# A decoder layer on one core: the cross norm's statistics, its powers and xn's transposes moved to later places

## The chip, the core and the metric

One core of a Trainium2 chip runs the whole layer in one program. The metric is the device time of one execution in microseconds; lower is better. The engines are TensorE (PE in the profile, its weight loads PEld), VectorE (DVE), ScalarE (ACT), GpSimd (POOL) and SyncE (SP, which here only issues DMAs). Each engine takes its instructions in the order of the program, and they meet through semaphores.

## The reference, cut to what is computed

B = 16 sequences of T = 256 tokens with D = 256 features and H = 16 heads of 16.

```
x = layernorm(x + attn(x))                 # causal self attention, q and k rms-normed and rotated
x = layernorm(x + xattn(x, ctx, mask))     # causal cross attention on ctx
x = layernorm(x + ffn(x))                  # ffn(x) = heavy(x) + light(x); with n = 256 all tokens are routed
feedforward: h = x / max(|x|, 1e-12) * sqrt(D) * gamma;  gelu(h @ w1.T + b1) @ w2.T + b2
```

The steps around the change are the second layer norm and the normalisation at the head of the FFN: `x2 = (y2 - mean) * rstd`, then `xn = x2 * rr2`, where `rr2` comes from the variance and `rstd` alone (`ss2 = var * rstd * rstd`, then a power of -1/2).

## The kernel before

The kernel is software-pipelined over the 16 sequences. `iterations` calls `step(i)` for i from -2 to 19 on each engine, and in a step four sequences are at work: `s = i` (self attention), `c = i - 1` (cross attention), `f = i - 2` (end of cross attention, second norm, xn) and `l = i - 3` (FFN). `live(b)` is true where the sequence exists. The sequence f exists together with s in the 14 steps i = 2 to 15, and without s in the steps 16 and 17.

On TensorE a step has four stages of 16 heads each: self scores, `scores(1, s, h)`; cross scores, `scores(2, c, h)`; transposed self scores, `scores_t(1, s, h)`; transposed cross scores, `scores_t(2, c, h)`. Everything else that TensorE does is put ahead of a given head by a list of positions: `phase` issues, at each h, first the "others" of that position and then the head. Three PSUM banks go round as a ring for the heads: `wait_ring` makes a head wait until the maximum (first two stages) or the exponential (last two) of the head three earlier has read its bank. `values(a, b, gr)` multiplies four masked heads by v; in the third stage it stands ahead of the heads 7, 11 and 15 (`VALUES_AFTER = 7`, every 4), and it waits for the masks of its four heads. `ffn_out` matmuls fill the third stage ahead of the heads 0 to 10.

A head of the third stage goes through three engines: TensorE scores it, ScalarE takes its exponential (`exponential`, line 768), GpSimd zeroes the causal half (`mask_probs`, line 1311), TensorE multiplies it by v (`values`). `mask_probs(a, b, between)` can run another function ahead of the mask of a given head: `between[h]()`.

The second norm runs like this. VectorE adds the residual (`add_residual(2, f, ...)`), takes the statistics (`statistics(2, f)`: two bn_stats, line 1022, two bn_aggr, line 1028), GpSimd adds epsilon and takes the power (`inverse_deviation(2, f)`, lines 1269 and 1290) and derives the second factor (`inverse_norm2(f)`, lines 1276, 1279, 1282 and 1290), VectorE scales (`layer_norm(2, f)`, line 1043; `scale2(f)`, line 1052), TensorE transposes xn (`transpose_xn`, line 397), ScalarE copies the high half from the bank (`copy_xn`), VectorE takes the low half (`low_xn`, line 1112). All in one step. Both halves feed `hidden` of the next step; `qk1(i + 2, 1)` at head 6 of the fourth stage waits for `low_xn` as well, since both use bank 7.

In the kernel before, the statistics stand ahead of the maximum of cross head 6 in the second stage (`STAT2_AT = 6`); GpSimd does `inverse_deviation(2, f)` and `inverse_norm2(f)` ahead of its first self mask; VectorE's order behind the cross maxima (`maxima`, `max_parts`) is layer_norm, max_t, the split of the next q (`split(1, i + 1, 0, 0)`), scale2, the split of the next k, low_xn, the third residual and its statistics, and the division of the self heads (`divide_pair`); TensorE transposes xn ahead of head 12 of the third stage (`XNT_AT = 12`); ScalarE copies it behind the exponential of self head 13.

Of the kernel before, what the change touches and what calls it, by code (L numbers as in the profile page):

```python
# [59 lines left out]
FCH = 9  # L60
# [5 lines left out]
def build(nc, io):  # L66
# [4 lines left out]
    with ctx:  # L71
# [144 lines left out]
        def live(b):  # L216

            return not isinstance(b, int) or 0 <= b < B
# [149 lines left out]
        def _(pe):  # L368
# [257 lines left out]
            def step(i):  # L626
                s, c, f, l = i, i - 1, i - 2, i - 3

                others = {}

                def add(at, fn, *args):
                    others.setdefault(at, []).append(lambda: fn(*args))

                if live(c):
                    add(X1T_AT, transpose_x1, c)
                if live(f):
                    add(OUT2_AT[0], values, 2, f, NG - 1)
                if live(c):
                    add(Q2_AT, q2, c)
                if live(f):  # L640
                    add(OUT2_AT[1], out_tokens, f)
                    add(OUT2_AT[2], out_dims, f)
                    add(OUT2_AT[3], out_proj, 2, f)
                if live(l):
                    for j in range(FCH):
                        add(HIDDEN_AT[j], hidden, l, j)
                phase((lambda h: scores(1, s, h)) if live(s) else None, others)

                others = {}
                if first(i + 1):  # L650
                    add(0, qk1, i + 2, 0)
                    add(0, qk1, i + 2, 1)
                if live(i + 1):
                    add(QKT_AT, transpose_qk1, i + 1)
                if live(s):
                    add(MAX1_AT, transpose_max, 1, s)
                if live(c):
                    add(V2_AT, v2, c)
                if live(l):
                    for j in range(FCH):  # L660
                        add(FFN0_AT[j], ffn_out, l, 0, j)
                phase((lambda h: scores(2, c, h)) if live(c) else None, others)

                others = {}
                if live(c):
                    add(MAX2_AT, transpose_max, 2, c)
                if live(f):
                    add(XNT_AT, transpose_xn, f)
                if live(l):
                    for j in range(FCH):  # L670
                        add(FFN1_AT[j], ffn_out, l, 1, j)
                if live(s):
                    for gr in range(NG - 1):
                        add(HG * gr + VALUES_AFTER, values, 1, s, gr)
                phase((lambda h: scores_t(1, s, h)) if live(s) else None, others)

                others = {}
                if live(s):
                    add(K2_AT, k2, s)
                    add(OUT1_AT[0], values, 1, s, NG - 1)  # L680
                if live(i + 2) and not first(i + 1):
                    add(QK1_AT[0], qk1, i + 2, 0)
                if live(i + 2) and not first(i + 1):
                    add(QK1_AT[1], qk1, i + 2, 1)
                if live(s):
                    add(OUT1_AT[1], out_proj, 1, s)
                if live(i + 2):
                    add(V1_AT, v1, i + 2)
                if live(c):
                    for gr in range(NG - 1):  # L690
                        add(HG * gr + VALUES_AFTER, values, 2, c, gr)
                phase((lambda h: scores_t(2, c, h)) if live(c) else None, others)
# [7 lines left out]
        def _(act):  # L700
# [92 lines left out]
            def step(i):  # L793
# [38 lines left out]
                for h in range(H):  # L832
                    if live(s):
                        if h % HG == 0 and h >= 2 * HG:
                            copy_group(1, s, h // HG - 2)
                        exponential(1, s, h)
                    if h == COPY_XN_AT and live(f):
                        copy_xn(f)

                for h in range(H):  # L840
                    if live(s):
                        if h == COPY1_AT[0]:
                            copy_group(1, s, NG - 2)
                        if h == COPY1_AT[1]:
                            high_part(2, s, 1, 0)
                        if h == COPY1_AT[2]:
                            copy_group(1, s, NG - 1)
                    for t in range(TT):
                        if h == SQ_AT[t] and live(i + 2) and not first(i + 1):
                            squares(i + 2, t)  # L850
                    if live(c):
                        if h % HG == 0 and h >= 2 * HG:
                            copy_group(2, c, h // HG - 2)
                        exponential(2, c, h)
                    if h == COPY_V1_AT and live(i + 2):
                        copy_v(1, i + 2)
# [44 lines left out]
        def _(dve):  # L901
# [213 lines left out]
            def step(i):  # L1115
# [40 lines left out]
                def statistics_cross():  # L1156
                    if live(f):
                        statistics(2, f)

                if live(c):  # L1160
                    maxima(2, c, {RESID2_AT: residual_cross, MAXT_AT: max_rows, STAT2_AT: statistics_cross})
                    max_parts(2, c)
                else:
                    residual_cross()
                    max_rows()
                    statistics_cross()

                if live(f):
                    layer_norm(2, f)
                if live(c):  # L1170
                    max_t(2, c)
                if live(i + 1):
                    split(1, i + 1, 0, 0)
                if live(f):
                    scale2(f)
                if live(i + 1):
                    split(1, i + 1, 1, 1)
                if first(i):
                    scale_w1()
                if live(f):  # L1180
                    low_xn(f)
                if live(l):
                    dve.wait_ge(s_x2b, l + 1)
                    add_residual(3, l, FFN_BANK, x2b)
# [1 line left out]

                if live(s):
                    divide_pair(s, 0)
                    take_rest(2, s, 1, 0)
                    divide_pair(s, 1)  # L1190
                    split_rest(2, s, 1, 0)
# [58 lines left out]
        def _(pool):  # L1250
# [63 lines left out]
            def step(i):  # L1314
# [39 lines left out]
                if live(i - 4) and i - 4 < B - 1:  # L1354
                    layer_norm3(i - 4)

                if live(f):
                    inverse_deviation(2, f)
                    inverse_norm2(f)

                if live(s):
                    mask_probs(1, s, {})

                roots = {}
                if live(l):
# [36 lines left out]
HIDDEN_AT = (6, 6, 8, 8, 11, 11, 14, 14, 16)  # L1402
QKT_AT, MAX1_AT, V2_AT = 2, 4, 6
FFN0_AT = (3, 5, 7, 8, 9, 10, 11, 12, 13)
MAX2_AT, XNT_AT = 5, 12
FFN1_AT = (0, 1, 2, 3, 4, 6, 8, 9, 10)
K2_AT, OUT1_AT, QK1_AT, V1_AT = 1, (3, 9), (3, 6), 13

MIDQ_AT, COPY2_AT, COPY_XN_AT, COPY_V1_AT = 1, 4, 13, 15
COPY1_AT, SQ_AT = (0, 3, 3), (5, 7)  # L1410
QN_AT, NORM2_AT, SPLITQ_AT, LOWQ_AT, RESID2_AT, MAXT_AT, STAT2_AT = (1, 2), 5, 6, 8, 1, 3, 6
RSTD3_AT, RSTD1_AT = 3, 13
NSTK = (None, 2 * len(TERMS_Q), 2 * len(TERMS_Q) + 1)
NEWTON = 3 + 3 * 3
N_SELF, N_CROSS, N_FFN = 3, 5, 8
# [44 lines left out]
```

## Time and profile before

| | |
|---|---|
| median of 3 runs | 978.58 us (974.46 to 981.06) |
| profiled execution | 978.16 us, of which its span is 976.4 us |
| busy share of the span | PE 91%, PEld 71%, DVE 74%, ACT 51%, POOL 55% |
| granted TensorE clock, mean | 0.960 of full speed |

The span reaches from the first to the last instruction. The shares are means over a start, some 13 steps that look alike, and an end. Times in rows are microseconds from the start of the span; a row of the timeline gives start, duration, engine, line, operation, tiles and, in brackets, the idle time just before it and what ended it. A count such as x4 merges instructions that follow each other.

### The profile page before, as it was taken

Reading aid. Unit: us, or ns where it says so; the run is one execution under the profiler, and the core shown is the slowest. Engines: PE = TensorE matmul, PEld = TensorE weight load, DVE = VectorE, ACT = ScalarE, POOL = GpSimd, SP = SyncE. Lnnn points to the kernel's source line nnn. Section 1 sums busy time; section 2 is a strip of 40 time slices with the busy share of each in tenths; the row PEclk is TensorE's granted clock in tenths of the full one; section 3 lists DMA queues with packets and bytes.
Section 4 is the critical chain, followed back from the end, with each engine's and each line's share of the span. In section 5 each row is a group of like instructions: output and inputs, shape, how many; then the busy total and the mean of one; then the engine's idle time right before and its main releaser. Section 6 shows DMA issues by size and latency. Waiting matters only on the chain. (4 is left out here: it accounts for less than half of the span.)

```text
span 976.4 us, 21698 instructions
## 1 busy us (share of the span) xinstructions
PE 888.3 (91%) x7712; PEld 689.7 (71%) x7712; DVE 725.3 (74%) x1764; ACT 496.8 (51%) x1063; POOL 537.9 (55%) x1047
## 2 busy tenths in 40 slices
PE   3367897999999999999999999999999999999886
PEld 2335565787868787777878787877778686767576
DVE  7788687878788878879787888788887877663411
ACT  1132444646475655656464756556464746455332
POOL 7554465646564756656565647657565656162421
PEclk9669898999999999999999999999999999999888
DMA  3794383727476654818275666738283656613000
GB/s 110 120 173 68 52 110 50 106 33 109 51 100 78 98 78 65 111 37 110 34 119 59 100 78 80 97 54 107 44 109 42 95 72 88 77 31 49 14 11 21
DMA packets 79644, 74.22 MB, mean 76 GB/s; under 512 B 8593, under 2 KB 78897, under 8 KB 79537
## 3 DMA queue, kind: packets, MB, share of 16 engines
q1 hardware_dynamic: 75008, 68.11, 50.5%
q10 hardware_dynamic: 4528, 4.73, 1.9%
q8 instruction: 61, 1.00, 0.5%
q14 instruction: 47, 0.38, 0.2%
HBM read 17.49 MB, written 4.20 MB: 22 GB/s over the span
## 5 line engine op out<-in xcount | busy, mean ns | idle before, releaser
L768 ACT ACTIVATE pr<-bank 128x384 f32<-128x384 f32 x512 | 240.0, 500 | 188.1 <-PE bank L370 187.0
L946 DVE TENSOR_REDUCE mx<-bank 128x3 f32<-128x384 f32 x512 | 266.4, 552 | 89.7 <-PE bank L370 87.5
L1311 POOL TENSOR_SCALAR_AFFINE_SELECT pr<-pr 128x256 f32<-128x256 f32 x512 | 222.1, 448 | 132.3 <-ACT pr L768 130.1
L370 PE MATMUL bank<-w,g 128*128 128x256 f32 x576 | 170.8, 389 | 1.1 <-ACT g L780 1.1
L370 PE MATMUL bank<-cmaskb,idb 128*128 128x256 bf16 x512 | 143.3, 280 | 27.7 <-DMA stk2k<-nat1k 13.7
L780 ACT ACTIVATE g<-bank,b 128x256 f32<-128x256 f32 x144 | 67.8, 473 | 83.5 <-PE bank L370 83.2
L1335 POOL TENSOR_TENSOR xTlow<-xT,xThigh 128x512 fp32r<-128x512 f32 x16 | 20.8, 1301 | 149.8 <-ACT xThigh L702 149.8
L370 PEld LDWEIGHTS bank<-w,g 128*128 128x128 f32 x576 | 89.6, 190 | 5.2 <-ACT g L780 1.5
L370 PEld LDWEIGHTS bank<-cmaskb,idb 128*128 128x128 bf16 x512 | 50.1, 98 | 50.5 <-DVE mx L946 22.5
L370 PE MATMUL bank<-stk2k,stk2q 97*128 97x128 bf16 (+1 forms) x512 | 85.1, 253 | 0.0
L370 PE MATMUL bank<-stk1q,stk1k 100*128 100x256 bf16 (+1 forms) x512 | 80.1, 254 | 2.4 <-DMA stk1q<-mT 1.0
L370 PE MATMUL bank<-stk1k,stk1q 97*128 97x128 bf16 (+1 forms) x512 | 80.6, 246 | 0.0
L370 PE MATMUL bank<-stk2q,stk2k 100*128 100x256 bf16 (+1 forms) x512 | 69.1, 255 | 5.3 <-DMA stk2q<-mT 3.6
L264 POOL TENSOR_TENSOR qc<-qn,ropeC 128x256 f32<-128x256 f32 x60 | 49.3, 821 | 43.8 <-DVE qn L1087 43.8
L370 PE MATMUL bank<-xnh,w1h 128*128 128x256 f32 x288 | 66.6, 313 | 3.7 <-DVE y L1015 2.1
L370 PEld LDWEIGHTS bank<-stk1q,stk1k 100*128 100x128 bf16 x512 | 42.4, 100 | 36.7 <-issue 7.5
L370 PEld LDWEIGHTS bank<-stk2k,stk2q 97*128 97x128 bf16 x512 | 51.9, 101 | 19.3
L370 PE MATMUL bank<-wo,onT 128*128 128x256 f32 x256 | 63.0, 390 | 1.3 <-DVE onT L997 1.3
L370 PE MATMUL bank<-pr,va 128*32 128x256 f32 (+1 forms) x1024 | 57.5, 344 | 3.7 <-POOL pr L1311 3.5
L370 PE MATMUL bank<-xnl,w1h 128*128 128x256 f32 x288 | 58.3, 284 | 0.0
L370 PE MATMUL bank<-xnh,w1l 128*128 128x256 f32 x288 | 58.2, 284 | 0.0
L370 PEld LDWEIGHTS bank<-stk2q,stk2k 100*128 100x128 bf16 x512 | 36.4, 100 | 30.8 <-issue 15.1
(166 smaller groups left out, 1832.5 us busy)
## 6 DMA issues: line engine op xcount, KB each, us to landing
stk1q<-nat1q SPq DMA_DIRECT2D x90, 128.0 KB, 4.5
stk1k<-nat1k SPq DMA_DIRECT2D x90, 128.0 KB, 5.4
stk2k<-nat2k SPq DMA_DIRECT2D x90, 128.0 KB, 4.6
stk2q<-nat2q SPq DMA_DIRECT2D x90, 128.0 KB, 5.7
xT<-in_xT SPq DMA_DIRECT2D x16, 256.0 KB, 5.9
ctxT<-in_ctxT SPq DMA_DIRECT2D x16, 256.0 KB, 6.0
x<-in_x SPq DMA_DIRECT2D x16, 256.0 KB, 5.7
out_x<-x SPq DMA_DIRECT2D x16, 256.0 KB, 2.2
```

The costliest lines, as they stand in the source:

```text
L264: ops.tensor_tensor(qc[:, t, s * D:(s + 1) * D].rearrange("p (h d) -> p h d", d=HD), qn[:, t, s * D:(s + 1) * D].rearrange("p (h d) -> p h ...
L370: return nc.tensor.matmul(out, lhsT, rhs, start=start, stop=stop, skip_group_check=check)
L768: nc.scalar.activation(pr[:, h % (2 * HG), :], ring_bank("T", a, b, h)[:, 0:3 * P], ACT.Exp, scale=HD ** -0.5)\
L780: nc.scalar.activation(g[:, j, :], bank[HIDDEN_BANK[j % 2]][:, 0:T], ACT.Gelu, bias=b1[:, j:j + 1])\
L946: V.tensor_reduce(mx3[:, h, :], scored[:, 0:3 * P].rearrange("p (k t) -> p k t", k=3), AX.X, ALU.max, negate=True).then_inc(s_mx[a], 1)
L1311: G.affine_select(out=slot, in_=slot, compare_op=ALU.is_ge, fill=0.0, base=0, pattern=[[0, 2], [1, P]], channel_multiplier=-1).then_inc(s_ ...
L1335: G.tensor_tensor(xTp[1][:, :, :], xT[:, :, :], xTp[0][:, :, :].bitcast(f32), ALU.subtract)\
```

## The change

- VectorE: `statistics_cross` is called behind `max_parts(2, c)` and no longer between the maxima; `layer_norm(2, f)` goes behind `max_t` and the split of the next q, `scale2(f)` behind the split of the next k, `low_xn(f)` behind the third norm's statistics and `divide_pair(s, 0)`.
- GpSimd: `inverse_deviation(2, f)` goes from ahead of the self masks to ahead of the mask of self head 2, `inverse_norm2(f)` to ahead of that of head 5. Where there is no s, both stay where they were.
- TensorE: `transpose_xn(f)` goes from ahead of head 12 of the third stage to the head of the fourth, ahead of its first head. Where there is no s it stays at position 12.
- ScalarE: `copy_xn(f)` goes from behind self exponential 13 to ahead of cross exponential 1; where there is no s, to the first position of the self loop.

No operation is added or taken away, and no DMA is touched.

```diff
 # TensorE
-                if live(f):
-                    add(XNT_AT, transpose_xn, f)
+                if live(f) and not live(s):
+                    add(FCH + 3, transpose_xn, f)
 ...
                 others = {}
+                if live(f) and live(s):
+                    add(XNT_AT, transpose_xn, f)
 # ScalarE
-                    if h == COPY_XN_AT and live(f):
+                    if h == 0 and live(f) and not live(s):
                         copy_xn(f)
                 for h in range(H):
+                    if live(f) and live(s) and h == COPY_XN_AT:
+                        copy_xn(f)
 # VectorE
-                    maxima(2, c, {RESID2_AT: residual_cross, MAXT_AT: max_rows, STAT2_AT: statistics_cross})
+                    maxima(2, c, {RESID2_AT: residual_cross, MAXT_AT: max_rows})
                     max_parts(2, c)
                 else:
                     residual_cross()
                     max_rows()
-                    statistics_cross()
-                if live(f):
-                    layer_norm(2, f)
+                statistics_cross()
                 if live(c):
                     max_t(2, c)
                 if live(i + 1):
                     split(1, i + 1, 0, 0)
                 if live(f):
-                    scale2(f)
+                    layer_norm(2, f)
                 if live(i + 1):
                     split(1, i + 1, 1, 1)
+                if live(f):
+                    scale2(f)
                 if first(i):
                     scale_w1()
-                if live(f):
-                    low_xn(f)
                 if live(l):
                     ...
                 if live(s):
                     divide_pair(s, 0)
+                if live(f):
+                    low_xn(f)
+                if live(s):
                     take_rest(2, s, 1, 0)
 # GpSimd
+                roots = {}
                 if live(f):
-                    inverse_deviation(2, f)
-                    inverse_norm2(f)
-
+                    roots[RSTD2_AT[0]] = lambda: inverse_deviation(2, f)
+                    roots[RSTD2_AT[1]] = lambda: inverse_norm2(f)
                 if live(s):
-                    mask_probs(1, s, {})
+                    mask_probs(1, s, roots)
+                else:
+                    for h in sorted(roots):
+                        roots[h]()
 # positions
-MAX2_AT, XNT_AT = 5, 12
+MAX2_AT, XNT_AT = 5, 0
-MIDQ_AT, COPY2_AT, COPY_XN_AT, COPY_V1_AT = 1, 4, 13, 15
+MIDQ_AT, COPY2_AT, COPY_XN_AT, COPY_V1_AT = 1, 4, 1, 15
-RSTD3_AT, RSTD1_AT = 3, 13
+RSTD2_AT, RSTD3_AT, RSTD1_AT = (2, 5), 3, 13
```

## Rows read from the trace of the kernel before

**Rows 1.** Windows: third stage of step 7, busy time by engine, granted clock.

```profile
429.42:439.72 10.30, 10.15 (x104) 6.83 (x102) 7.32 (x19) 7.54 (x18) 8.58 (x20) 1.00 0.42 81
```

**Rows 2.** Waits of PE over ten like steps, 240.6 to 781.3.

```profile
PE bank L397 <- DVE x L1043: 2.9, 10, 0.3
PE bank L370 <- DVE mx L946: 1.9, 10, 0.3
PE bank L370 <- POOL pr L1311: 0.6, 3, 0.2
```

**Rows 3.** Timeline of DVE in step 7, second and third stage.

```profile
422.66 0.73 DVE L1022 BATCH_NORM_STATS2 st<-y 128x6 f32<-128x256 f32 x2
423.32 0.29 DVE L1028 BATCH_NORM_AGGREGATE mv<-st 128x2 f32<-128x6 f32 x2
...
427.92 0.56 DVE L946 TENSOR_REDUCE mx<-bank 128x3 f32<-128x384 f32 x1 [0.15 <-PE bank L370]
...
431.23 0.75 DVE L1043 TENSOR_SCALAR x<-y,mv,rstd 128x256 f32<-128x256 f32 x2
...
434.17 0.77 DVE L931 TENSOR_TENSOR nat1q<-rest,nat1q 128x512 bf16<-128x512 f32 x1
```

**Rows 4.** Timeline of POOL in step 7, third stage.

```profile
429.28 0.22 POOL L1269 TENSOR_SCALAR ve<-mv 128x2 f32<-128x2 f32 x1
429.58 0.71 POOL L1290 TENSOR_TENSOR rstd<-ve,minus_half 128x2 f32<-128x2 f32 x1
430.36 0.19 POOL L1276 TENSOR_TENSOR part<-mv,rstd 128x2 f32<-128x2 f32 x1
...
431.32 0.72 POOL L1290 TENSOR_TENSOR rr<-ssm,minus_half 128x2 f32<-128x2 f32 x1
432.01 0.41 POOL L1311 TENSOR_SCALAR_AFFINE_SELECT pr<-pr 128x256 f32<-128x256 f32 x1
...
433.09 0.41 POOL L1311 TENSOR_SCALAR_AFFINE_SELECT pr<-pr 128x256 f32<-128x256 f32 x1
...
434.36 0.85 POOL L1311 TENSOR_SCALAR_AFFINE_SELECT pr<-pr 128x256 f32<-128x256 f32 x1
...
436.58 0.57 POOL L1311 TENSOR_SCALAR_AFFINE_SELECT pr<-pr 128x256 f32<-128x256 f32 x1 [0.24 <-ACT pr L768]
...
437.24 0.72 POOL L1311 TENSOR_SCALAR_AFFINE_SELECT pr<-pr 128x256 f32<-128x256 f32 x1
...
438.29 0.41 POOL L1311 TENSOR_SCALAR_AFFINE_SELECT pr<-pr 128x256 f32<-128x256 f32 x1 [0.34 <-ACT pr L768]
```

**Rows 5.** Timeline of ACT in step 7: the exponential of self head 11.

```profile
437.74 0.49 ACT L768 ACTIVATE pr<-bank 128x384 f32<-128x384 f32 x1 [0.57 <-PE bank L370]
```

**Rows 6.** Timeline of PE in step 7: self values, xn's transposes.

```profile
433.55 0.86 PE L370 MATMUL bank<-pr,va1b 128*32 128x256 f32 x16
...
436.57 0.86 PE L370 MATMUL bank<-pr,va1b 128*32 128x256 f32 x16
...
437.54 0.61 PE L397 MATMUL bank<-idf,xn 128*128 128x128 f32 x4
437.98 0.66 PE L370 MATMUL bank<-stk1q,stk1k 100*128 100x256 bf16 x6
438.75 0.86 PE L370 MATMUL bank<-pr,va1b 128*32 128x256 f32 x16
```

**Rows 7.** Timeline of step 16, the first without self heads: PE, then DVE.

```profile
915.03 0.60 PE L397 MATMUL bank<-idf,xn 128*128 128x128 f32 x4
916.59 0.67 PE L370 MATMUL bank<-stk1q,stk1k 100*128 100x256 bf16 x6 [0.97 <-DMA stk1q<-mT]
...
912.84 0.73 DVE L1043 TENSOR_SCALAR x<-y,mv,rstd 128x256 f32<-128x256 f32 x2
```

**Rows 8.** Windows of step 15, fourth stage: before the clock falls, and after.

```profile
871.30:878.20 6.90, 5.11 (x64) 3.47 (x61) 6.66 (x16) 5.33 (x15) 4.75 (x12) 1.00 0.32 59
878.20:881.60 3.40, 3.40 (x8) 2.60 (x9) 0.90 (x2) 0.35 (x1) 1.17 (x2) 0.50 0.58 110
```

## The prediction, made before the result was known

> **What bounds the kernel now.** I read the busy shares first, then one like step in four windows, then the waits of TensorE over ten steps, then the timelines of the four engines in the third stage, where three of the four edits act. TensorE is busy 91% of the span, and in the third stage of step 7 it is busy 10.15 us of 10.30 at a granted clock of 1.00 [rows 1]. Its waits over ten steps come to 2.9 + 1.9 + 0.6 = 5.4 us [rows 2]. So in the middle of the program the end is set by TensorE's own work, and the most that any order of the other engines can give back there is about 0.54 us a step: over the 14 steps in which f and s are both there 7.6 us, 0.8%. An edit here can lose far more than it can win: whatever makes TensorE wait longer adds to the end directly, since later stages have no slack in which the loss could go.
>
> What the reader is to see in the third stage is how near GpSimd is to TensorE. The mask of self head 3 ends at 433.09 + 0.41 = 433.50 [rows 4] and the first values start at 433.55 [rows 6]: they start 0.05 us behind the mask, which is to say that the masks already end last there.
>
> **VectorE: statistics behind the maxima.** In the loop they cost 422.66 to 423.61, 0.95 us [rows 3]. Taking them out of the second stage gains nothing, because behind them VectorE sits idle 0.15 us ahead of a maximum and TensorE ends that idle time [rows 3]: the maxima are paced by TensorE there, and `max_parts` ends when it did. The statistics then take the slot of the scaling that starts at 431.23 [rows 3], so the means and variances are ready at 431.23 + 0.95 = 432.18, where they were ready at 423.61. `max_t`, whose copy is next in the queue, waits for transposes on TensorE anyway, and the 0.95 us take the place of 0.75 us of scaling [rows 3]; no cost. The later places of `layer_norm`, `scale2` and `low_xn` cost nothing either: xn is wanted only at the head of the fourth stage, and VectorE sat idle for xn's copy before. If that cover were gone, the cost would be one scaling, 0.75 us.
>
> **GpSimd: the powers between the masks.** This is where I see the price. GpSimd works in order. Ahead of the mask of head 2 it now waits for the statistics, at 432.18, plus some 0.07 us for the semaphore (my estimate, near the 0.05 us between mask and values): 432.25. Epsilon and power take 429.28 to 430.29, 1.01 us [rows 4], so they end at 433.26, and the mask of head 2 starts at 433.22 (it starts a little ahead of the end of the power before it, as at 432.01 [rows 4]). Before, the chain was done at 432.04, and the first mask started at 432.01. Masks of a queue that is behind follow each other by (433.09 - 432.01) / 3 = 0.36 us [rows 4], so the mask of head 3 ends at 433.22 + 0.36 + 0.41 = 433.99 and the first values start at 434.04 where they started at 433.55: 0.49 us lost. Behind the waiting instruction are queued the masks of all heads from 2 on; who waits for them is TensorE, with everything that follows.
>
> The second factor comes ahead of head 5: from the start of line 1276 to the next mask it is 430.36 to 432.01, 1.65 us [rows 4]. Now the mask of head 4 starts at 433.95 and runs beside the subtraction of line 931 (434.17 to 434.94 [rows 3]). Masks are longer in some places: 0.85 us at 434.36, which is beside that very line, 0.57 and 0.72 at 436.58 and 437.24, against 0.41 [rows 4]. With 0.57 for head 4, the chain starts at 434.59 and the mask of head 5 at 436.24; head 6 follows at 436.60. The second split, with line 931 again, now falls there, so I give head 6 0.57 and head 7 0.72: the end is 436.60 + 0.57 + 0.72 = 437.89, and the second values start at 437.94 where they started at 436.57 [rows 6]. That is 1.37 us, and it holds the first 0.49. The ends: with every mask at 0.41, head 4 ends at 434.36, the chain starts at 434.43, head 5 at 436.08, head 7 ends at 436.08 + 0.36 + 0.36 + 0.41 = 437.21: 0.69 us lost. With 0.85 for the heads 4, 6 and 7, the chain starts at 434.87, head 5 at 436.52, head 6 at 436.88, and head 7 ends at 438.58: 2.06 us lost. I take 1.37, since 0.57 and 0.72 are what the masks beside the second split took.
>
> A rule of the skill bears on the chain itself. The scaling of line 1043 now runs beside it, and before it also ran beside it: from 431.23 to 431.98 [rows 3], while the power of line 1290 took 0.72 us at 431.32 against 0.71 at 429.58 [rows 4]; the row shows no cost. The Trainium skill, GPSIMD Engine Reference, section "Key points", says that GpSimd shares its SBUF interfaces with VectorE and that they contend when VectorE runs an instruction in a two-port mode or with two SBUF inputs. By the rule a scaling like line 1043 could hold the small operations up to its 0.75 us, which would add 0.75 x 14 = 10.5 us to the end and lead to the upper end of my range; by the row nothing, which I take. For the long masks beside line 931, which has two SBUF inputs, rule and rows agree.
>
> **TensorE: the transposes at the head of the fourth stage.** The work is the same, 0.44 us from 437.54 to 437.98 [rows 6], but it leaves a place where TensorE has too little to do. The third values wait for the mask of head 11: its score comes behind the second values, its exponential runs 437.74 to 438.23 [rows 5], its mask 438.29 to 438.70 [rows 4], and the values start at 438.75 [rows 6], 2.18 us behind the second ones. This chain has no transposes in it. Without them TensorE reaches the same wait 0.44 us sooner and starts the third values no sooner; behind the third stage the 0.44 us come on top. So 0.44 us a step. What would keep that from happening is other filler between the heads 11 and 15; the program has none there.
>
> **ScalarE: the copy of xn ahead of cross exponential 1.** In the fourth stage TensorE runs `k2` between the cross heads 0 and 1, so ScalarE has a hole of the size of the copy there; `qk1(i + 2, 1)` wants `low_xn` only at head 6. Nothing. No DMA queue is passed: SP's loads wait for things that do not move.
>
> **Where there is no s.** In step 16 the chain is bare: statistics from 912.84 [rows 7], ready at 913.79, power done 1.08 us later at 914.87, second factor 1.69 us (430.36 to 432.04 [rows 4]) later at 916.6, `scale2` as long as the scaling, 0.73 [rows 7], done at 917.3. The transposes were at 915.03, and the cross heads began at 916.59 when a DMA of the maxima landed [rows 7]. Now transposes and heads come at about 917.4 and 917.8: 1.2 us, and the copy of xn now stands between them and the first exponential: 0.3 more. I take 1.5 us (1.2 to 1.8). Step 17 has no cross maxima; VectorE's new order there costs or gains 0.1 us.
>
> **The sum.** A step loses 1.37 + 0.44 = 1.81 us; 14 steps lose 25.3; with step 16 it is 26.8. The profiled execution took 978.16 us, 1.76 outside its span, close to the median of 978.58. So 978.16 + 26.8 = 1005. The ends: (0.69 + 0.44) x 14 + 1.2 = 17, which gives 995; (2.06 + 0.44) x 14 + 1.8 = 36.8, which gives 1015. 1% of this kernel is about what a measurement can tell from no change, here 968.8 to 988.4.
>
> **Rivals.** First, on the other side: not slower. The mechanism is the statistics coming early enough: if VectorE, relieved of 0.95 us, ran its last maxima and `max_parts` sooner, the variances would be there when GpSimd has masked heads 0 and 1, at about 431.4, and the masks would run ahead of where they were. It decides from 0.8 us sooner than my 432.18. Then only the 0.44 us stays, less the little that TensorE waits for masks now: some 0.3 us x 14 + 1.5 = 5.7, near 983 to 984. For it: VectorE does lose 0.95 us of work ahead of the place. Against it: the 0.15 us of idle time behind the statistics [rows 3], which say that TensorE sets the pace. Chance 0.12.
>
> Second, the clock. In step 15 TensorE was busy 5.11 us of 6.90, and then the granted clock fell from 1.00 to 0.50, so to 1.2 GHz, for 3.4 us [rows 8], in which a full clock would have done the work in 1.7. The new waits spread over the third stage. If the clock fell once in every step there, it would cost 1.7 x 14 = 24 us more: 1029. For it: the new waits lie within a few us, as those did. Against it: there the idle share was 1.79 of 6.90 us, 26%, and here it is 0.15 + 1.37 + 0.44 = 1.96 us of a third stage of 10.30 - 0.44 + 1.81 = 11.7 us, 17%. The Trainium skill, TensorE: Matmul & The Clock Gate, section "HAM oscillation — how this bites in real kernels", tells of kernels whose waits drop the clock again in every tile; by it this is the case to fear. Chance 0.13.
>
> Third, the transposes: if the third values turn out not to wait for head 11's mask alone, the 0.44 us are not lost, and it is 1.37 x 14 + 1.5 = 20.7: 999. That lies within the forecast's range.
>
> **How the numbers follow.** The forecast of slower, 995 to 1015, has 0.68; not slower 0.12; the clock 0.13; the rest, 0.07, lies between (a part of the masks' delay, 985 to 995) or, 0.03 of it, below 968.8, for which I know no mechanism, since 0.8% is all there is to win. The range of 983 to 1015 holds the forecast, the first rival and what lies between, and leaves the clock out. Slower by over 1%: 0.68 + 0.13 + 0.04, 0.85; within 1%: the first rival, 0.12; faster: 0.03.
>
> **What would show it.** After the change the waits of TensorE for GpSimd's masks should grow from 0.6 us over ten steps to over 10; line 1269 for the second norm should show idle time ended by line 1028; the first and the second values should come some 0.5 and 1.4 us later behind the start of the third stage; the third ones 2.18 us behind the second with a wait ahead of them; like steps should be 1.8 us longer. Wrong would be: variances ready well before 432.2 on this scale, masks of 0.41 throughout, or a granted clock of 0.5 in the middle of the program.

## The result, and the profile after

The changed kernel took 1011.65 us, median of 4 runs (1008.05 to 1015.15), against 979.55 (974.46 to 981.06, 4 runs) of the kernel before: a ratio of 1.0337, with a 95% interval of 1.0280 to 1.0394. Slower, as forecast; the forecast was 1005, so it is 6.65 us more than that. The profiled execution took 1008.05 us, with a span of 1006.3 and a mean granted clock of 0.962.

The busy times, from the page of the kernel after:

```profile
PE 890.4 (88%) x7712; PEld 688.5 (68%) x7712; DVE 726.8 (72%) x1764; ACT 498.1 (49%) x1063; POOL 538.8 (54%) x1047
```

TensorE's share falls from 91% to 88% with the same instructions: it waits more. For whom, the waits of TensorE say, over ten like steps of the kernel after (252 to 817; total us, times, longest).

```profile
PE bank L370 <- POOL pr L1316: 19.1, 20, 1.6
PE bank L397 <- DVE x L1047: 2.9, 10, 0.3
PE bank L370 <- ACT pr L770: 2.5, 10, 0.3
PE bank L370 <- DVE mx L950: 1.9, 10, 0.3
```

Against [rows 2] the waits for VectorE are as they were, the wait for the masks (line 1316, once 1311) has gone from 0.6 to 19.1, twice a step, and a wait of 0.25 for an exponential is new. Windows over the four stages of step 7 give 14.96, 11.66, 12.69 and 17.09 us, before 14.96, 11.66, 10.30 and 17.08: only the third stage has grown. This is its window, with the columns of [rows 1]:

```profile
441.62:454.31 12.69, 10.39 (x103) 6.82 (x102) 11.49 (x32) 7.72 (x18) 8.93 (x21) 1.00 0.55 86
```

Where the time goes in it, the timelines of step 7 show. The third stage starts at 441.62, where it was 429.42, so 12.20 us are to be taken off for a comparison with the rows of before. First GpSimd in the kernel after:

```profile
442.55 0.41 POOL L1316 TENSOR_SCALAR_AFFINE_SELECT pr<-pr 128x256 f32<-128x256 f32 x1 [1.16 <-ACT pr L770]
...
444.84 0.22 POOL L1274 TENSOR_SCALAR ve<-mv 128x2 f32<-128x2 f32 x1 [1.24 <-DVE mv L1032]
445.14 0.71 POOL L1295 TENSOR_TENSOR rstd<-ve,minus_half 128x2 f32<-128x2 f32 x1
445.81 0.62 POOL L1316 TENSOR_SCALAR_AFFINE_SELECT pr<-pr 128x256 f32<-128x256 f32 x1
446.39 0.85 POOL L1316 TENSOR_SCALAR_AFFINE_SELECT pr<-pr 128x256 f32<-128x256 f32 x1
447.20 0.45 POOL L1316 TENSOR_SCALAR_AFFINE_SELECT pr<-pr 128x256 f32<-128x256 f32 x1
447.62 0.23 POOL L1281 TENSOR_TENSOR part<-mv,rstd 128x2 f32<-128x2 f32 x1
...
448.58 0.85 POOL L1295 TENSOR_TENSOR rr<-ssm,minus_half 128x2 f32<-128x2 f32 x1
449.40 0.45 POOL L1316 TENSOR_SCALAR_AFFINE_SELECT pr<-pr 128x256 f32<-128x256 f32 x1
```

GpSimd has masked head 0, sits idle for 1.24 us until the variances come (1274, the old 1269), takes the power, and masks the heads 2, 3 and 4 in 0.62, 0.85 and 0.45. VectorE beside it, kernel after:

```profile
442.64 0.35 DVE L970 CAST mp<-nm 128x32 bf16<-128x32 f32 x1
443.25 0.38 DVE L974 CAST mp<-nr 128x32 bf16<-128x32 f32 x1
443.78 0.75 DVE L1026 BATCH_NORM_STATS2 st<-y 128x6 f32<-128x256 f32 x2
444.44 0.30 DVE L1032 BATCH_NORM_AGGREGATE mv<-st 128x2 f32<-128x6 f32 x2
...
445.74 0.43 DVE L928 CAST nat1q<-rest 128x512 bf16<-128x512 f32 x1
446.20 0.77 DVE L935 TENSOR_TENSOR nat1q<-rest,nat1q 128x512 bf16<-128x512 f32 x1
```

Two things are to be seen. The masks of heads 0 and 1 (442.55 and 443.20) lie over the two casts of `max_parts`, which take 0.35 and 0.38; so the statistics start at 443.78 and the variances are there at 444.74, 0.36 later than the 432.18 + 12.20 = 444.38 of the prediction. And the masks of heads 2 and 3 lie over the cast and the subtraction of the split. TensorE, kernel after:

```profile
447.29 0.86 PE L370 MATMUL bank<-pr,va1b 128*32 128x256 f32 x16 [1.58 <-POOL pr L1316]
...
450.72 0.86 PE L370 MATMUL bank<-pr,va1b 128*32 128x256 f32 x16 [0.33 <-POOL pr L1316]
451.51 0.67 PE L370 MATMUL bank<-stk1q,stk1k 100*128 100x256 bf16 x6
452.43 0.34 PE L370 MATMUL bank<-stk1q,stk1k 100*128 100x256 bf16 x2 [0.25 <-ACT pr L770]
452.90 0.86 PE L370 MATMUL bank<-pr,va1b 128*32 128x256 f32 x16
...
453.87 0.61 PE L397 MATMUL bank<-idf,xn 128*128 128x128 f32 x4
454.31 0.33 PE L370 MATMUL bank<-stk2q,stk2k 100*128 100x256 bf16 x2
```

Taking off 12.20 us and [rows 6], the first values come 447.29 - 12.20 - 433.55 = 1.54 us later, the second ones 1.95, the third ones 1.95, and the fourth stage starts 454.31 - 12.20 - 439.72 = 2.39 later.

To put the whole span together I take TensorE's first transpose of the maxima in each step (line 532) as a marker. From step 2's to step 15's it is 730.50 us, before 700.80: 29.70 for 13 steps, of which the steps 3 to 13 have 2.35 each (25.89 / 11). Step 15 adds 0.70. The start adds 0.48, and all behind the cross maxima of step 16 is 62.45 us instead of 63.43, 0.98 less. The sum is 29.90 = 1006.3 - 976.4.

### The profile page after: what moved, and what is told of

It is laid out like the page before. It is cut to its first block, busy times and chain, and to the rows that moved or that the text cites. A ratio compares the mean times of both kernels' runs of the same rounds, so it can differ in the third digit from the quotient of the medians.

```text
span 1006.3 us, 21698 instructions
## 1 busy us (share of the span) xinstructions
PE 890.4 (88%) x7712; PEld 688.5 (68%) x7712; DVE 726.8 (72%) x1764; ACT 498.1 (49%) x1063; POOL 538.8 (54%) x1047
## 4 chain that ended last, share of the span: by engine, by line
PE 50%; DVE 24%; POOL 12%; issue 6%; ACT 4%; DMA 3%; ACTq 0%; POOLq 0%; SPq 0%; DVEq 0%
PE bank L370 48%; DVE mx L950 10%; POOL pr L1316 6%; POOL rstd L1295 2%; PE bank L397 2%; ACT pr L770 2%; DVE qn L1091 2%; DVE x L1047 1%; POOL rr L1295 1%; DMA stk2k<-nat1k 1%; DMA stk2q<-nat2q 1%; DVE nt L1081 1%; DVE rest L921 1%; ACT nat2q L704 1%; DVE mp L974 1%
## 5 line engine op out<-in xcount | busy, mean ns | idle before, releaser
L1316 POOL TENSOR_SCALAR_AFFINE_SELECT pr<-pr 128x256 f32<-128x256 f32 x512 | 224.4, 456 | 136.5 <-ACT pr L770 136.2
L1340 POOL TENSOR_TENSOR xTlow<-xT,xThigh 128x512 fp32r<-128x512 f32 x16 | 20.3, 1269 | 150.6 <-ACT xThigh L704 150.6
L370 PE MATMUL bank<-wo,onT 128*128 128x256 f32 x256 | 61.4, 382 | 0.0
```

Source lines behind the costliest of these rows:

```text
L370: return nc.tensor.matmul(out, lhsT, rhs, start=start, stop=stop, skip_group_check=check)
L1316: G.affine_select(out=slot, in_=slot, compare_op=ALU.is_ge, fill=0.0, base=0, pattern=[[0, 2], [1, P]], channel_multiplier=-1).then_inc(s_ ...
L1340: G.tensor_tensor(xTp[1][:, :, :], xT[:, :, :], xTp[0][:, :, :].bitcast(f32), ALU.subtract)\
```

## The experiments

The theory that the trace suggests (it is called A in the expectations): three delays in the third stage add up, all by the order in GpSimd's and TensorE's queues. The first power waits for late statistics, and the masks behind it collide with the split; the second factor's chain goes ahead of head 5; the transposes leave a hole ahead of the third values. Its rivals: VectorE's new order costs by itself, or the waits cost through the clock. The first four kernels undo one part of the change or make one alone.

**Transposes and copy of xn back in the third stage**, all else as changed:

```diff
-                if live(f) and not live(s):
+                if live(f):
                     add(FCH + 3, transpose_xn, f)
...
-                if live(f) and live(s):
-                    add(XNT_AT, transpose_xn, f)
```

(FCH + 3 is position 12; `copy_xn` went back behind self exponential 13.)

> The changed kernel with xn's transposes back ahead of head 12 of the third stage and xn's copy back behind self exponential 13; everything else as changed. Theory A (GpSimd's wait for the late statistics holds up the masks, and the transposes cost only their own 0.44 us a step as lost filler): 14 x 0.44 = 6 us under the changed kernel's 1011.65, about 1005, and the second values still some 1.9 us late. Rival B (the place of the transposes is the main cost): under 990. Rival C (the clock falls in each step because of the waits): no part of this run, the clock stays at 1.00 in the middle as in the changed kernel.

Measured: 1003.86 us (1002.22 to 1004.98), ratio 1.0261 [1.0221, 1.0302] to 979.3 of the kernel before. Like steps are 55.97 us, against 56.40 changed: 0.43 less. TensorE's timeline of this kernel in step 7:

```profile
449.83 0.61 PE L397 MATMUL bank<-idf,xn 128*128 128x128 f32 x4
...
451.05 0.86 PE L370 MATMUL bank<-pr,va1b 128*32 128x256 f32 x16
```

The transposes again fill the hole, and the wait of 0.25 us for an exponential, which the changed kernel has ahead of the third values, is gone. The term of 0.44 us a step is shown by the like steps. The medians lie 7.8 us apart, against 0.44 x 14 = 6.2; falls of the clock in the middle, of which this execution has two, spread them (below).

**Statistics back among the cross maxima**, the powers still between the masks:

```diff
-                    maxima(2, c, {RESID2_AT: residual_cross, MAXT_AT: max_rows})
+                    maxima(2, c, {RESID2_AT: residual_cross, MAXT_AT: max_rows, STAT2_AT: statistics_cross})
...
-                statistics_cross()
```

> The changed kernel with the cross statistics back ahead of the maximum of cross head 6; everything else as changed. Theory A: the variances are there before the masks begin, so GpSimd does not wait ahead of head 2; what stays is 0.44 us of lost filler and up to 0.4 us for the second factor ahead of head 5, 0.4 to 0.9 us a step: 985 to 992. Rival B (the transposes are the main cost): 1000 or more. Rival D (the masks are slow because of VectorE's split beside them, not because of the wait): still over 1000, with masks of 0.6 to 0.85 ahead of the first values.

Measured: 997.29 us (996.30 to 998.82), ratio 1.0201 [1.0167, 1.0235]. That is 14.4 us better than changed, but longer than A had expected. The first values are back (3.66 us behind the first self exponential, 3.76 before), so all of their delay hung on the wait for the late statistics. But the second values are 1.18 us later than before. GpSimd's timeline of this kernel shows why:

```profile
444.27 0.42 POOL L1280 TENSOR_TENSOR part<-mv,rstd 128x2 f32<-128x2 f32 x1
444.77 0.65 POOL L1283 TENSOR_TENSOR ss<-part,rstd 128x2 f32<-128x2 f32 x1
445.51 0.26 POOL L1286 TENSOR_SCALAR ssm<-ss 128x2 f32<-128x2 f32 x1
445.92 0.73 POOL L1294 TENSOR_TENSOR rr<-ssm,minus_half 128x2 f32<-128x2 f32 x1
446.61 2.94 POOL L1315 TENSOR_SCALAR_AFFINE_SELECT pr<-pr 128x256 f32<-128x256 f32 x6
```

VectorE's timeline beside it, same kernel:

```profile
444.21 0.43 DVE L928 CAST nat1q<-rest 128x512 bf16<-128x512 f32 x1
444.67 0.69 DVE L935 TENSOR_TENSOR nat1q<-rest,nat1q 128x512 bf16<-128x512 f32 x1
```

Now the chain lies over the split, and its first two operations take 0.42 and 0.65 us instead of some 0.2; the chain is 446.61 - 444.27 = 2.34 long, where it was 1.65. Both operations of GpSimd that lie beside it took longer. A's expectation had given the second factor up to 0.4 us, which left this out.

**The powers later**, ahead of the heads 4 and 8, so just behind the masks that the first and the second values want:

```diff
-RSTD2_AT, RSTD3_AT, RSTD1_AT = (2, 5), 3, 13
+RSTD2_AT, RSTD3_AT, RSTD1_AT = (4, 8), 3, 13
```

> The changed kernel with the power ahead of the mask of self head 4 (was 2) and the second factor ahead of that of head 8 (was 5); statistics stay behind the maxima. Theory A: the first values come no later than in the kernel before, since four masks run before GpSimd meets the wait; the second factor now falls ahead of the masks of the third values and can cost up to 0.5 us there: 0.4 to 0.9 us a step with the transposes, 985 to 994. Rival B or a cost of VectorE's new order: 1005 to 1012, no change, since only GpSimd's positions differ.

Measured: 992.84 us (990.20 to 994.25), ratio 1.0151 [1.0114, 1.0187]; like steps 55.27, so 1.2 us longer than before, where 0.4 to 0.9 had been expected. With the late statistics and VectorE's new order untouched, the first values start 3.66 us behind the first exponential and the second ones 6.68 (before 3.76 and 6.78). The delay is now at the third values only. ScalarE's first exponential, GpSimd's first power and TensorE's three groups of values in step 7, from the timelines of this kernel:

```profile
438.19 0.49 ACT L770 ACTIVATE pr<-bank 128x384 f32<-128x384 f32 x1 [4.79 <-PE bank L370]
...
441.21 0.22 POOL L1274 TENSOR_SCALAR ve<-mv 128x2 f32<-128x2 f32 x1
...
441.85 0.86 PE L370 MATMUL bank<-pr,va1b 128*32 128x256 f32 x16
...
444.88 0.86 PE L370 MATMUL bank<-pr,va1b 128*32 128x256 f32 x16
...
447.98 0.86 PE L370 MATMUL bank<-pr,va1b 128*32 128x256 f32 x16 [1.06 <-POOL pr L1316]
```

Line 1274 starts right behind the fourth mask, with no wait ahead of it: when GpSimd comes to the power here, the variances are there. So late variances cost nothing in themselves; what costs is which masks are queued behind the wait for them. What is left at the third values, 0.82 us, goes with longer powers ahead of their masks, 0.90 and 1.08 us in place of 0.71. Of the loss of 32.1 us, 18.6 hang on two numbers in a list (13.5 are left).

**The transposes alone**, in the kernel before (with the copy ahead of cross exponential 1, and `low_xn` behind the division):

```diff
-                if live(f):
+                if live(f) and not live(s):
                     add(XNT_AT, transpose_xn, f)
...
+                if live(f) and live(s):
+                    add(0, transpose_xn, f)
```

> The kernel before with nothing but xn's transposes at the head of the fourth stage, xn's copy ahead of cross exponential 1 and the low half behind the first division; statistics and powers stay. Theory A: the third values wait 0.44 us more and the transposes come on top, 14 x 0.44 = 6 us over the kernel before: about 986. If the transposes were hidden in either place: 979.6, no change. Rival B: over 1000.

Measured: 981.34 us (976.71 to 985.12, 10 runs), ratio 1.0035 [1.0009, 1.0061]: 2 us, where 0.44 x 14 = 6.2 had been expected. Like steps are 54.5 to 54.7, so 0.5 longer in the middle, as it should be; step 14 (52.38 against 52.79) and step 15 with step 16's head (60.84 against 61.33) give 0.9 back, and behind the maxima of step 16 it is 60.0 us instead of 63.4. In this kernel the loss in the middle is seen in full in the steps, and only in part in the time.

The other six kernels take up the collision, GpSimd's order, VectorE's order, and the clock.

**The collision**: in the changed kernel, `layer_norm(2, f)` ahead of the first split, so that the split falls later than the masks 2 to 4.

```diff
-                if live(i + 1):
-                    split(1, i + 1, 0, 0)
                 if live(f):
                     layer_norm(2, f)
+                if live(i + 1):
+                    split(1, i + 1, 0, 0)
```

> The changed kernel with VectorE's layer_norm(2, f) ahead of the first split instead of behind it, so that the split's last subtraction no longer runs beside the masks of heads 2 and 3 but later. Theory D (that subtraction stretches those masks): the masks of heads 2 and 3 at 0.36 to 0.5 us each, the first values 0.4 to 0.6 us sooner than in the changed kernel; the split then falls on the second factor's chain, so the second values gain at most 0.3 us: 1007 to 1013. If the long masks have another cause: the first values no sooner.

Measured: 1014.45 us (1010.93 to 1015.74), ratio 1.0382 [1.0354, 1.0410] to 976.35; above the 1007 to 1013 expected, and not told apart from the changed kernel. But the places have changed, as GpSimd's timeline of this kernel shows in a like step:

```profile
735.08 0.41 POOL L1316 TENSOR_SCALAR_AFFINE_SELECT pr<-pr 128x256 f32<-128x256 f32 x1
735.44 0.46 POOL L1316 TENSOR_SCALAR_AFFINE_SELECT pr<-pr 128x256 f32<-128x256 f32 x1
...
736.27 0.19 POOL L1281 TENSOR_TENSOR part<-mv,rstd 128x2 f32<-128x2 f32 x1
...
737.32 1.08 POOL L1295 TENSOR_TENSOR rr<-ssm,minus_half 128x2 f32<-128x2 f32 x1
738.37 2.96 POOL L1316 TENSOR_SCALAR_AFFINE_SELECT pr<-pr 128x256 f32<-128x256 f32 x6
```

The masks of heads 2 and 3 take 0.41 and 0.46, and the first values come 0.62 us sooner than in the changed kernel: the collision is shown. Now the split lies over the chain, the power takes 1.08, and the second values come 0.22 later than in the changed kernel, where at best a small gain had been expected. The contention was moved, and not taken away.

**Both powers ahead of all masks, late statistics kept.** This takes the interleaving out of the change and leaves its lateness:

```diff
-                    mask_probs(1, s, roots)
-                else:
-                    for h in sorted(roots):
-                        roots[h]()
+                    for h in sorted(roots):
+                        roots[h]()
+                    mask_probs(1, s, {})
```

(The loop over `roots` stands ahead of the branch in the kernel, for both cases.)

> The changed kernel with both powers ahead of all self masks, as in the kernel before, while the statistics stay behind the maxima: the suspected wait at its largest. Theory A: the first mask starts only behind the whole chain, the first values some 3.3 us later than in the kernel before, with the transposes 3.7 us a step: about 1033. If GpSimd's wait is not what costs: 1012, as the changed kernel.

Measured: 1073.59 us (1073.41 to 1075.74), ratio 1.0998 [1.0972, 1.1024], 40 us above the expectation. Windows of this kernel, before and in the stretch in which the clock falls:

```profile
463.20:468.20 5.00, 2.01 (x15) 1.23 (x12) 4.44 (x12) 2.04 (x5) 3.76 (x9) 1.00 0.32 94
468.20:475.10 6.90, 5.62 (x30) 3.28 (x30) 1.81 (x5) 1.75 (x4) 3.62 (x8) 0.51 0.79 90
```

TensorE waits 4.27 us for the masks (first values 4.24 us later than before), is busy for 2.01 us of 5.00, and then the clock is at 0.51 for 6.9 us; from step 4 on it falls so in every like step. Steps are 61.4 us, and from the first to the second values it is 5.68 us, where it was 436.57 - 433.55 = 3.02. Here the clock rival of the prediction happens in full. TensorE's wait, from its timeline of this kernel:

```profile
469.48 1.51 PE L370 MATMUL bank<-pr,va1b 128*32 128x256 f32 x16 [4.27 <-POOL pr L1316]
```

In this kernel no mask runs beside `max_parts`, and its two casts take 0.18 us each, as in the kernel before. The statistics then start 462.91 - 461.12 = 1.79 us behind the start of the third stage, and in the changed kernel 443.78 - 441.62 = 2.16. So the lateness of the variances comes and goes with the masks beside the casts.

**Both powers in GpSimd's idle time**: the kernel before, with `inverse_deviation(2, f)` and `inverse_norm2(f)` ahead of the subtraction that makes the low half of x (`xTlow`).

```diff
+                if live(f) and live(s):
+                    inverse_deviation(2, f)
+                    inverse_norm2(f)
...
-                if live(f):
+                if live(f) and not live(s):
```

> The kernel before with both powers ahead of GpSimd's xTlow, where it sits idle some 10 us a step; nothing else moved. Theory A: the masks begin right behind the first exponential, the first values start some 0.1 us sooner, 14 x 0.1 = 1.4 us: 978, no difference that a measurement tells. If early powers were worth more than that, 974 or less.

Measured: 972.23 us (971.43 to 974.78, 9 runs), ratio 0.9961 [0.9946, 0.9977] to 976.35 (18 runs). GpSimd's timeline:

```profile
424.00 0.22 POOL L1269 TENSOR_SCALAR ve<-mv 128x2 f32<-128x2 f32 x1 [9.80 <-DVE mv L1028]
```

The chain follows the statistics at once, in a place where GpSimd has sat idle for 9.80 us; the first values start 3.66 us behind the first exponential instead of 3.76, and like steps are 53.88 us instead of some 54.07. That is more than the 0.1 us a step that had been expected, and the time lies below the 974 that was set as the mark for it. In the kernel before, TensorE waited some 0.2 us for the masks in three of ten like steps [rows 2]; here it does in none.

**The same, with a filler moved**: the last `ffn_out` pair of the third stage at head 13 rather than 10.

```diff
-FFN1_AT = (0, 1, 2, 3, 4, 6, 8, 9, 10)
+FFN1_AT = (0, 1, 2, 3, 4, 6, 8, 9, 13)
```

> The same and the last ffn_out matmul pair of the third stage ahead of head 13 in place of head 10, so that TensorE has more to do in the fixed 2.18 us between second and third values: the reverse of what the change did with the transposes. If filler there is what counts, the third values come some 0.3 us sooner, with the 0.1 us 0.4 us a step: about 974. If TensorE has no time left there: 978.

Measured: 972.29 us (968.69 to 975.67, 10 runs), ratio 0.9958 [0.9934, 0.9982]. Steps are 53.73, another 0.15 less, which the medians of the two don't tell apart. The 2.18 us from the second to the third values turn out not to be fixed: without the filler ahead of them the second values come 0.49 us sooner (6.19), and the third ones follow 2.49 us behind them with no wait, 0.18 sooner than in the kernel above (8.68 against 8.86). Both are faster than either kernel, by 0.4% of the kernel before.

**VectorE's order alone.** From the changed kernel, the statistics back among the maxima and the powers in GpSimd's idle time; what remains of the change are the later places on VectorE and the transposes and copy:

```diff
+                if live(f) and live(s):
+                    inverse_deviation(2, f)
+                    inverse_norm2(f)
...
-                if live(f):
+                if live(f) and not live(s):
                     roots[RSTD2_AT[0]] = lambda: inverse_deviation(2, f)
```

> The changed kernel with the statistics back in the maxima and both powers ahead of GpSimd's xTlow where it is idle; what is left of the change is VectorE's later layer_norm, scale2 and low_xn, and the transposes and the copy in the fourth stage. If VectorE's later places cost nothing, as I said: only the 0.44 to 0.5 us of lost filler stays, less 0.1 for the early powers: 0.4 us a step over the kernel before, 979 to 985, first and second values 0.1 us sooner than in the kernel before. If they cost something: over 988.

Measured: 976.18 us (974.37 to 981.03, 10 runs), ratio 1.0024 [1.0002, 1.0046] to 973.64 (13 runs). First and second values come at 3.66 and 6.68 us, and steps are 54.35: against the 53.88 of the kernel with the powers in idle time they have 0.47 more, which is the transposes' hole. For VectorE's new order next to nothing is left, and that rival falls. The time lies below the 979 to 985 expected, but the kernel before was faster in this comparison too. By their ratios to it, this kernel and the one with the powers in idle time are 0.63% apart, some 6 us, so here 0.47 x 14 = 6.6 us of steps are seen in the time.

**The changed kernel once more**, for the clock:

> The changed kernel itself once more, for the clock: its four runs lay between 1008 and 1015 with mean clocks of 0.962 and 0.952, and its profiled run, the fastest, shows no fall of the clock in the middle. If the clock is what parts the runs, a profile of a slower one shows falls to 0.50 of 3.4 us each in the middle, with steps about 1.5 us longer there; if not, steps of 56.4 us throughout and the time lost elsewhere.

Measured: 1014.62 and 1009.20 us, ratio 1.0378 [1.0314, 1.0442]. In the profiled one of 1014.62 the clock falls three times in the middle; windows ahead of the first fall and in it:

```profile
273.00:280.00 7.00, 5.42 (x44) 3.86 (x45) 6.53 (x19) 3.43 (x7) 4.31 (x10) 1.00 0.13 43
280.00:283.40 3.40, 3.40 (x25) 1.99 (x14) 2.65 (x6) 1.25 (x3) 2.91 (x8) 0.50 0.99 152
```

The falls lie at 280.0, 563.3 and 846.6. The steps with the first two are 57.6 us instead of 56.4, and the third's is 55.6, where the same step had 54.4: 1.2 us each. The first profiled execution had none in the middle and took 1008.05. Three falls, 3.6 us, are about half of the 6.57 us between the two; of the rest, 1.53 us lie up to the end of step 2, and 1.53 behind the maxima of step 16.

## Why the prediction was right, and where it was off

**Right in kind.** Each of its three delays is in the trace, and each goes away when its part is undone: the masks behind the first power (statistics back, or powers later: first values at 3.66), the chain ahead of head 5 (powers later: second values at 6.68), the transposes (put back: steps 0.43 shorter). The waits for masks grew to 19.1 us over ten steps (over 10 had been said), line 1274 waits for line 1032, and the third values start 452.90 - 450.72 = 2.18 us behind the second ones, as worked out. The wait that shows there is not for the mask of head 11 alone: 0.25 us of it is for an exponential, ahead of the scores of head 14, which come before the values.

**The step that was mis-sized** is the first term under "GpSimd: the powers between the masks": 0.49 us lost at the first values; it was 1.54. Of the missing 1.05 us, 0.39 is the start of the mask of head 2 (445.81 against 433.22 + 12.20 = 445.42): the variances were 0.36 late, since the casts of `max_parts` doubled beside masks that did not run there before. I had priced the masks beside VectorE, and not VectorE beside the masks. The other 0.66 is the length of the masks of heads 2 and 3: that of head 3 ends at 447.24, and 433.99 + 12.20 = 446.19 had been worked out. I priced the masks of heads 2 and 3 at the 0.36 us and 0.41 us of a free queue and put the subtraction of the split beside head 4; but the cast ahead of it, which I had left out, fell on head 2, and the subtraction on head 3. In step 15 of the changed kernel itself there is no next q to split: there the three masks behind the power take 1.22 us together (1.84 in step 7), and the wait of the first values is 0.97 instead of 1.58. With the kernel that moves the norm ahead of the split, this is shown twice.

**Partly offset at the second values.** From the first to the second values I had 3.90 us; it was 450.72 - 447.29 = 3.43, as the heads 4 to 7 took 0.45 each, and not 0.57 and 0.72 for some. So the delay is 1.95 against 1.37, and with 0.44 for the transposes 2.39 a step against 1.81. That is 0.58 x 14 = 8.1 us more than the sum. Measured were 32.1 us between the medians and 29.9 between the spans, against 26.8 forecast: 5.3 and 3.1 more. The rest of the 8.1 was returned outside the like steps, mainly by the end, priced at 1.5 us lost and measured at 0.98 won, and by step 15, which lost only 0.70. None of this had been foreseen, so it is in part luck that the time lies this near to 1005.

**The chain's own price.** In step 7 of the changed kernel, from line 1281 to the next mask it is 449.40 - 447.62 = 1.78 us, against 1.65: near enough to what I took, because the first split had ended and the second came over the last power only (0.85). But the reason that I gave, no cost in the row, was read beside a scaling and holds no further: beside the split the chain took 2.34 us, and one power 1.08. The Trainium skill, GPSIMD Engine Reference, section "Key points", says that GpSimd contends with VectorE instructions of two SBUF inputs. The subtraction of the split is one, and with 0.65 us for an operation of some 0.2 beside it, the runs agree.

**Where there is no s.** From TensorE's transposes of the maxima in step 16 to the first cross heads it was 916.59 - 912.97 = 3.62 us [rows 7] and is now 948.71 - 943.85 = 4.86, so 1.24 more, and the next heads (917.51, now 949.94) come 1.55 later; 1.2 and 1.5 had been forecast. TensorE's timeline there, kernel before:

```profile
912.97 0.29 PE L532 MATMUL bank<-idb,mp 128*48 128x128 bf16 x2
```

Kernel after:

```profile
943.85 0.29 PE L532 MATMUL bank<-idb,mp 128*48 128x128 bf16 x2
...
948.22 0.66 PE L397 MATMUL bank<-idf,xn 128*128 128x128 f32 x4 [2.15 <-DVE xn L1056]
948.71 0.66 PE L370 MATMUL bank<-stk1q,stk1k 100*128 100x256 bf16 x6
949.94 1.65 PE L370 MATMUL bank<-stk1q,stk1k 100*128 100x256 bf16 x8 [0.57 <-ACT pr L770]
```

And yet the tail is 0.98 us shorter. Behind these heads the clock falls in both kernels; the window of the half clock (0.50, so 1.2 GHz), kernel after:

```profile
950.30:957.10 6.80, 5.72 (x47) 2.38 (x48) 0.05 (x1) 3.80 (x10) 4.78 (x13) 0.50 0.01 2
```

The same window in the kernel before:

```profile
919.10:932.80 13.70, 11.02 (x90) 5.63 (x91) 0.40 (x2) 6.92 (x16) 8.27 (x18) 0.50 0.01 1
```

It lasts 6.80 us instead of 13.70, so the 1.5 us were lost there and won back behind. This gain is not shown to be the change's: the kernel with the powers in idle time, in which nothing moves where there is no s, has a fall of 6.8 us here too, and the second profiled execution of the changed kernel, with the same fall and one more, took 63.98 us for this tail, 0.55 more than the kernel before. What decides the length of the fall was not tried; it stays open.

**The rivals.** "Not slower" needed variances at 431.4; they came at 444.74 - 12.20 = 432.54: it fell, by TensorE's pace in the maxima. The third, transposes that cost nothing, fell when they were put back. The clock came in some steps of some executions, for 1.2 us each, and not in every step. My reason against it, that less of the stage is waited than ahead of the fall in [rows 8], did not exclude it: the stretch with 5.42 us busy of 7.00 was followed by a fall, and the same stretch of the next step (330.6 to 337.6, also 5.42 us busy) was not. In the kernel with both powers first the fall came in every like step from step 4 on, each time within a long wait for the masks (4.27 us; 3.09 in step 15). The Trainium skill, TensorE: Matmul & The Clock Gate, section "HAM oscillation — how this bites in real kernels", tells of a kernel whose waits drop the clock again in every tile. The kernel with both powers first agrees with it, and most steps of the changed kernel do not.

## What to carry to other kernels

Where two engines are within 0.05 us of each other, lay the whole new order of both on one time axis before pricing it: an instruction that moves changes not only its own place but which long operation of the neighbour it lies beside, and either of the two can get longer. A small chain belongs into an idle stretch of its own engine behind its producer (here 9.80 us were free), and if it must stand between the items of a queue, then just behind the item that the bottleneck is waiting for, and not ahead of it. And a loss counted in like steps is the loss of the middle only: the end differed by 1.53 us between two executions of the same kernel.

## What the hardware showed that was not expected

- VectorE and GpSimd slow each other in both directions. A cast of 128x32 on VectorE took 0.35 and 0.38 us beside a mask, and 0.18 with none beside. In the whole trace of the kernel after, the 35 such casts with no mask beside them took 0.18 us each, and the 29 with one 0.27 to 0.42. A mask took 0.62 to 0.85 beside the split and 0.41 without; a 128x2 product 0.65 instead of 0.20, a 128x2 power 1.08 instead of 0.71. VectorE's bn_stats did not change: 0.41 to 0.43 us each, with a mask beside them or without.
- The granted clock's fall is no fixed property of a kernel: the same program showed none in the middle in one execution and three in another, 3.4 us each; in the kernel in which TensorE waits 4.27 us at a time it came in every like step from step 4 on, for 6.9 us.
